# The item list's four steps moved to later passes of the preparation, in a fused graph layer on one core

## The reference, cut to what matters

```python
xn = _layernorm(x)                                  # mean and variance of every row
# graph convolution; deg counts the edges into a node, and one more for itself
norm = dinv[src] * dinv[dst]                        # dinv = rsqrt(deg)
gnn = relu(segment_sum((xn @ W)[src] * norm[:, None], dst) + b)
x = x + gnn + _L0_mix_ref(xn[None], ...)[0]
x = x + _L0_ffn_ref(_layernorm(x)[None], ...)[0]    # 8 experts, 978 rows each at most
```

## Time and profile before

| | us |
|---|---|
| median of 3 runs | 2458.72 (2458.11 to 2458.78) |
| the profiled execution: its time | 2454.8 |
| its span, from the first to the last instruction | 2453.0 |
| busy in the span: PE, DVE, ACT, POOL | 2157.4, 1770.2, 1213.4, 366.4 |
| mean granted clock of TensorE | 0.954 |

### The profile page before, as it was taken

One profiled execution on the slowest core, in us unless ns is written; L12 is line 12 of the kernel. 1 busy time (PEld: TensorE's weight loads), 2 busy tenths in 40 slices (PEclk: granted clock), 3 DMA queues, 4 the chain that ended last, 5 costly groups with the idle time before them and its releaser, 6 DMA issues. The chain is left out here.

```text
span 2453.0 us, 41210 instructions
## 1 busy us (share of the span) xinstructions
PE 2157.4 (88%) x13789; PEld 1545.6 (63%) x13789; DVE 1770.2 (72%) x5676; ACT 1213.4 (49%) x2731; POOL 366.4 (15%) x396
## 2 busy tenths in 40 slices
PE   3739999998998999888899899999989995999997
PEld 2625655566666666666666666666656654999897
DVE  3564544478887888888888888866766754887886
ACT  0435544455555555555555555444444444655563
POOL 7100000001111111111111011100000002333432
PEclk7869999999999999999999999999999997999999
DMA  5000000000000000000000000000010004222220
GB/s 182 13 7 3 3 3 3 3 3 5 3 3 3 5 3 3 3 5 3 3 3 3 3 5 3 6 29 29 31 38 29 29 27 124 79 68 87 88 81 9
DMA packets 52135, 63.54 MB, mean 26 GB/s; under 512 B 15695, under 2 KB 44330, under 8 KB 51808
## 3 DMA queue, kind: packets, MB, share of 16 engines
q1 hardware_dynamic: 27104, 29.06, 3.7%
q0 software_dynamic: 10336, 21.41, 3.2%
q10 hardware_dynamic: 14496, 10.53, 1.3%
HBM read 42.82 MB, written 20.92 MB: 26 GB/s over the span
## 5 line engine op out<-in xcount | busy, mean ns | idle before, releaser
L1189 PE MATMUL p_m<-node_halves,adj 128*128 128x512 f16 x3626 | 986.5, 389 | 17.1 <-DVE rows_v L1813 14.2
L1574 ACT CAST adj<-p_b 128x392 f16<-128x392 f32 x1184 | 570.0, 485 | 843.0 <-PE p_b L1179 827.7
L1786 DVE TENSOR_TENSOR one_src<-iota,codes 128x512 bf16<-128x512 bf16 x1184 | 503.8, 425 | 428.7 <-PE p_b L1179 418.8
L1179 PE MATMUL p_b<-one_edge,one_src 128*128 128x98 bf16 x4736 | 613.3, 266 | 54.8 <-ACT adj L1574 39.6
L1179 PEld LDWEIGHTS p_b<-one_edge,one_src 128*128 128x128 bf16 x4736 | 458.3, 116 | 298.9 <-DVE one_src L1786 61.9
L1189 PEld LDWEIGHTS p_m<-node_halves,adj 128*128 128x128 f16 x3626 | 360.1, 105 | 246.5 <-issue 41.4
L1786 DVE TENSOR_TENSOR one_edge<-iota,codes 128x392 bf16<-128x392 bf16 x1184 | 429.0, 362 | 0.0
L1103 POOL TENSOR_TENSOR x1r<-x1n,bc_ln1g 128x256 f32<-128x256 f32 x49 | 44.9, 916 | 840.1 <-ACT x1n L1498 840.1
L1092 POOL DMA_INDIRECT src_e<-in_srcR,item_chunk x37 | 38.2, 1033 | 727.8 <-DVEq L1808 726.3
L1156 POOL DMA_INDIRECT out_dram<-oo,slot_node x64 | 74.8, 1168 | 219.7 <-DVE oo L2210 203.1
L1138 POOL DMA_INDIRECT rows<-node_features,slot_row x64 | 73.2, 1144 | 165.7 <-DVE slot_node L2317 146.6
(11 more groups left out here) (343 smaller groups left out, 3530.9 us busy)
## 6 DMA issues: line engine op xcount, KB each, us to landing
w1raw<-in_w SPq DMA_DIRECT2D x8, 1024.0 KB, 5.3
w2raw<-in_w SPq DMA_DIRECT2D x8, 1024.0 KB
res<-in_x SPq DMA_DIRECT2D x7, 896.0 KB, 7.5
node_features<-res ACTq DMA_DIRECT2D x20, 256.0 KB
out_dram<-res ACTq DMA_DIRECT2D x20, 256.0 KB
out_dram<-res SPq DMA_DIRECT2D x1, 1152.0 KB
fb_b<-in_fb SPq DMA_DIRECT2D x1, 1024.0 KB, 9.2
rows<-node_features,slot_row POOLq DMA_INDIRECT x64, 4.9
```

The costliest lines, as they stand in the source:

```text
L1179: mm = pe.matmul(p_b[n % 2][:, u * HI2:(u + 1) * HI2], one_src[:, n % ONER, :, u], one_edge[:, n % ONER, :, u], start=True, stop=True)
L1189: mm = pe.matmul(p_m[:], adj[:, k % 2, h, :], node16[:, h, :], start=(h == 0), stop=(h == NBLK - 1))
L1574: nc.scalar.copy(adj[:, n // SPV % 2, :, n % SPV * 2 * IB:(n % SPV + 1) * 2 * IB] .rearrange("p h (u r) -> p h u r", r=2), p_b[n % 2][:, 0 ...
L1786: V.tensor_tensor(tile[:, n % ONER], iota4[:, 0:m, :], codes[:, q % 2, a, at:at + IB].rearrange("p (m u) -> p m u", m=1) .broadcast_to([P, ...
```

## The change

The four parts of the item list on TensorE stand ahead of the passes 10, 12, 14 and 17 (3, 6, 9 and 12 before). VectorE's steps are put in another order. Nothing is added or removed.

```diff
-    HIST_AT, TOTALS_AT, COUNTS_AT, SPREAD_AT = 3, 6, 9, 12
+    HIST_AT, TOTALS_AT, COUNTS_AT, SPREAD_AT = 10, 12, 14, 17
@@ VectorE's row of steps
-            statistics(0)
-            statistics(1)
+            for gi in range(4):
+                statistics(gi)
+            inverse_std(0)
             item_histogram()
-            statistics(2)
+            positions(0)
             item_totals()
-            statistics(3)
-            inverse_std(0)
-            positions(0)
+            statistics(4)
             item_chunks()
-            for gi in range(4, NG):
+            for gi in range(5, NG):
                 statistics(gi)
+            positions(1)
             item_places()
-            positions(1)
             inverse_std(1)
             inverse_std(2)
             scales(0)
```

## The result

| | before | after |
|---|---|---|
| median (runs) | 2458.72 us (2456.6 to 2459.61, 5 runs) | 2472.19 us (2468.42 to 2478.52, 5 runs) |
| ratio | | 1.0056 (95% interval 1.0044 to 1.0068) |
| span of the profiled execution | 2453.0 | 2470.4 |
| `degrees(0)` starts | 107.71 | 122.42 |
| first step of the second part (ScalarE, `xn_m`) | 159.96 | 173.76 |

The changed kernel is 13.5 us slower. The last row puts the loss into the preparation: it ends 173.76 - 159.96 = 13.8 us later. The span grew by 17.4, so 3.6 us of this profiled execution belong to the second part. Its length scatters, though its instructions are the same in every kernel here: over all kernels profiled for this document it lies between 2292 and 2301 us. I therefore compare the ends of the preparation first and the medians second.

A forecast was written before the change was run, and what follows sets the result against it. Until 82 us late TensorE signals (the hold) bound the preparation, then VectorE. `degrees(0)` 16.4 us later, less 1.7 given back, makes +14.7; on the median 2458.7 that is 2473.4 us, range 2462 to 2484.

The forecast's parts named there:

- The hold stays: Preparation up to 82 us: TensorE's signals come late while GpSimd issues 49 gathers; assumed as before, with statistics(2) and (3) inside.
- The histogram at 93.0: TensorE after the move: without `item_counts` ahead of it, pass 10's place is reached at 93.0 us instead of 93.59.
- first of the unknown costs: TensorE during the hold: it may get one pass further by 82 us, worth -2.2 us; taken as 0.
- TensorE waits 6.6 at `shift(0)`: TensorE, past pass 14 at 105.4 us, stands at `shift(0)` for `positions(1)` until 112.0.
- The pass behind it at half clock: TensorE's pass 15, after the wait at `shift(0)`, was to take 4.0 us instead of 2.16.
- VectorE waits 7.3 for the spread: VectorE's `item_places` waits from 112.4 us for `item_spread`, done at 119.7, with everything behind it: 7.3 us.
- 1.7 given back at the root: Behind `degrees(0)`: VectorE's 2.18 us wait for ScalarE's root falls to about 0.5, giving back 1.7 us.
- The later waits may shrink by up to 2: VectorE behind `degrees(0)`: the 3.8 us of waits there may shrink by up to 2; an unknown cost.
- A: Rival for the preparation: the hold is tied to the histogram's place and doesn't return; -36.5 us, 2422 us, chance 0.12.
- B: Rival for the preparation: the hold lets more through, TensorE four passes ahead at 82 us; +6.4, 2465 us, chance 0.08.
- C: Rival: no difference, as the later part would take up 10 us or more; about 2460 us, chance 0.04.
- D: Rival: the histogram's own signal is late by 13.3 us at the new place too; 2487 us, chance 0.04.

## Why the prediction was right

The time was forecast at 2473.4 us and is 2472.19; the +14.7 of the sum stand against +13.8 in the trace and +13.5 in the medians. That the time fits this closely is in part luck: the sum took the median to lie 3.9 us above the profiled execution, as before, and in the changed kernel the two are the same, while its second part was 3.6 us longer than before. The trace is the better test. The steps of the sum, one by one:

- *The hold stays, and the two groups of statistics run inside it.* Right. They did so in an odd manner: `statistics(2)` and `(3)`, 5.5 us of work, took from 27.99 to 54.5, most of it one instruction at a time (below). It cost nothing, as VectorE then waited another 28.59 us.
- *The histogram at 93.0.* It came at 91.13. TensorE was one pass ahead at 82 us: it ran one more from 37.54 to 42.04, within the stretch where the prediction called a busy TensorE a sign of being wrong. One pass ahead was the first of the unknown costs, named at -2.2 and taken as 0. This is the term that was off most: 1.9 us of the histogram's start, carried through to 1.7 at `degrees(0)` (122.42 against 124.1).
- *The wait for hist of "9 us or so"* was 7.40, from the same cause. *Short waits of 1.5 us each* were 1.67 and 1.92.
- *TensorE waits 6.6 at `shift(0)`.* 6.59. *The pass behind it at half clock, 4.0 us.* From 111.08 to 114.79, so 3.7. The granted clock fell to 0.79 on the mean from 110 to 120 us. The prediction called the pass at 126.56 the one row of that kind; the transposes of 1.09 us at 71.87, behind 40.22 us of standing, are another, and say the same. The Trainium skill (TensorE: Matmul & The Clock Gate, What's actually happening) has the throttled state as the default that activity lifts, and the trace agrees: 6.59 us of standing were followed by a slow pass; in the kernel with the spread ahead of pass 15 it was the spread that was slow, 1.90 us instead of 0.98.
- *VectorE waits 7.3 for the spread.* 7.64.
- *1.7 given back at the root.* 2.18 - 0.38 = 1.8. *The later waits may shrink by up to 2.* They grew a little: 1.20 and 2.83 us, where 0.78 and 2.33 stood, +0.9. With 14.7 at `degrees(0)` (122.42 - 107.71), -1.8 and +0.9 make the 13.8. So two terms were off, one by -1.7 and one by +0.9, and they partly cancel.

Of the rivals, A (the hold doesn't return) needed the histogram as the cause. The hold was there again with the histogram moved behind it, so the histogram isn't its cause. A's walk of the chain was sound all the same: it put `degrees(0)` of the changed kernel without a hold at 72.9, and on a free chip it starts at 72.74. Here too two errors cancel: the histogram came 1.1 us earlier than A had it, and the way from there to `degrees(0)` was 0.9 longer. But there the kernel before has no hold either, and the change costs 14.3 us as well. The sentence of the Trainium skill (SBUF — State Buffer, Who interferes with whom) that "PE and ACT never wait on anyone" stands in a list on the ports of the memory and says nothing of signals, so the prediction read more into it than is there. In the changed kernel, on a held chip, ScalarE's copy waited up to 30.44 us for a signal while GpSimd issued gathers; that isn't against the sentence, which is about something else. B had one pass ahead for its four; C needed the stretch behind `degrees(0)` to take up 10 us, and its waits grew instead; D's late signal at the new place isn't there, the copy of `hist` starts within 0.1 us of its matmuls' end.

## What to carry to other kernels

In a row of steps that each engine runs strictly in order, the place of the producer matters less than the consumer's place behind it: the same four parts, as late as in the changed kernel, cost 13.8 us of the preparation in one order of VectorE's row, and in another 0.7 us against the early places with a mended row of their own. Compare such a kernel with one that has the same mending, or the gain of the mending is put down to the move. Walk the row with durations, put each step that reads a result where that result is just done, and fill the time until then with steps that need nothing; when a wait goes, look at the next engine in the chain, since the wait for the root came back as 4.37 us when only `item_places` was moved. When a releaser can't be named and an engine far from the path issues a long run of gathers, cut the run with short pauses in a trial kernel before you move anything else: that was worth 28 us here in one execution on a held chip, more than any order of steps; on a free chip it brought nothing (ratio 1.0003), and it wasn't tried together with the better orders.

## What the runs showed of the hardware

- **Groups of executions differ by 2%.** The same program took 2458.7 and 2459.2 us in two groups and 2407.9 and 2407.4 us on two other chips, and the 50 us between them lie in one stretch of the preparation. A kernel is to be compared only with another of the same group, on the same chip.
- **Signals can come in steps.** During the hold, even VectorE's signals to itself can be late, and then come at distances of 0.7 us or its multiples. In the changed kernel, VectorE's aggregation of one group of statistics, 0.56 us elsewhere:

```profile
50.12 0.18 DVE L491 BATCH_NORM_AGGREGATE mv<-stats 128x2 f32<-128x6 f32 x1 [0.52 <-remote]
51.53 0.18 DVE L491 BATCH_NORM_AGGREGATE mv<-stats 128x2 f32<-128x6 f32 x1 [1.23 <-remote]
52.92 0.18 DVE L491 BATCH_NORM_AGGREGATE mv<-stats 128x2 f32<-128x6 f32 x1 [1.21 <-remote]
54.32 0.18 DVE L491 BATCH_NORM_AGGREGATE mv<-stats 128x2 f32<-128x6 f32 x1 [1.22 <-issue]
```

  The distances of the starts are 1.41, 1.39 and 1.40 us. On a free chip the seven take 0.56 us together. But not every signal in the hold is late: in the kernel before, right behind the copy of `hist` at 39.64, `statistics(2)` ran at full speed, between two waits of 11.56 and 39.28 us:

```profile
42.04 0.56 DVE L491 BATCH_NORM_AGGREGATE mv<-stats 128x2 f32<-128x6 f32 x7
```
- **Signals that had waited came in or just behind pauses of 1.7 to 1.8 us in GpSimd's gathers.** While it issues the next eight gathers, signals are late again (ScalarE waited 6.94 and 6.82 us in such runs). This is one execution, and each pause also waited for the gathers to land.
- **Thirteen of SyncE's loads have no part in it.** Moved behind the gathers, they changed nothing: 82.08 against 81.88 us for the copy of `totals` in one execution, and a ratio of 1.0001 on a free chip.
